# A three-layer cross network on one core: another order of GpSimd's additions, and other PSUM banks for ScalarE in layer 3

## The reference

```python
def cin_layer(xi, x0, W, b):            # xi (n, Fi, 32), x0 (n, 48, 32)
    Wr = W.reshape(Fi, 48, 128)
    out = einsum('nie,nje,ijo->noe', xi, x0, Wr) + b[None, :, None]
    return relu(out)
xs = [x0]
for W, b in ((W1, b1), (W2, b2), (W3, b3)):
    xs.append(cin_layer(xs[-1], x0, W, b))
z = concatenate(xs, axis=1).sum(axis=-1)
h = relu(concatenate([z, dense_ctx], 1) @ W_top1 + b_top1)
h = relu(h @ W_top2 + b_top2)
y = h @ W_top3
```

## Time and profile before

| | us |
|---|---|
| median of 3 runs (2476.27 to 2476.93) | 2476.67 |
| the profiled execution | 2476.69 |
| its span | 2474.9 |
| TensorE busy | 2330.4 (94%) |
| VectorE busy | 2277.5 (92%) |
| ScalarE busy | 2108.7 (85%) |
| GpSimd busy | 1904.7 (77%) |

### The profile page before, as it was taken

The page is one execution under the profiler, slowest core; times in us unless marked ns, Lnnn a source line. Parts: engine busy times, 40 slices in busy tenths (PEclk is TensorE's granted clock), DMA queues, the critical chain, the costliest instruction groups (busy, mean ns, idle before and its releaser), DMA issues.

```text
span 2474.9 us, 68697 instructions
## 1 busy us (share of the span) xinstructions
PE 2330.4 (94%) x14174; PEld 1177.3 (48%) x14174; DVE 2277.5 (92%) x9404; ACT 2108.7 (85%) x7910; POOL 1904.7 (77%) x1878
## 2 busy tenths in 40 slices
PE   1699999999999999999999999999999999999998
PEld 0355544454445544444454444444454555444443
DVE  6499999999999999999999999999999999999995
ACT  4589888898888988888988888888898898888884
POOL 7488888887778888888778888888777777777663
PEclk6799999999999999999999999999999999999999
DMA  5133333333333333333333333333333333333331
GB/s 168 28 69 71 70 70 62 70 71 68 60 70 70 71 61 70 71 65 66 69 68 71 66 66 70 67 64 70 67 66 64 69 69 68 68 61 68 68 60 37
DMA packets 150316, 168.61 MB, mean 68 GB/s; under 512 B 111956, under 2 KB 115671, under 8 KB 150264
## 3 DMA queue, kind: packets, MB, share of 16 engines
q0 software_dynamic: 43008, 137.39, 30.1%
q1 hardware_dynamic: 107256, 30.73, 5.6%
HBM read 12.82 MB, written 0.00 MB: 5 GB/s over the span
## 4 chain that ended last, share of the span: by engine, by line
DMA 23%; POOL 20%; PE 17%; ACT 16%; issue 13%; DVE 9%; DVEq 1%; ACTq 1%; POOLq 0%; SPq 0%
DMA work<-work 23%; PE y L469 13%; POOL part L346 12%; ACT work L567 11%; DVE acc L781 5%; POOL part L349 4%; PE m L459 3%; POOL psum L352 2%; ACT work L597 2%; POOL emb L294 2%; ACT zh L595 2%; DVEq L96 1%; ACT zst L592 1%; ACTq L96 1%; DVE mpw L822 0%
## 5 line engine op out<-in xcount | busy, mean ns | idle before, releaser
L469 PE MATMUL y<-whi,xT 128*128 128x512 f16 x6144 | 2009.5, 380 | 60.2 <-DVE acc L781 48.0
L567 ACT ACTIVATE work<-y,xc 128x128 f32<-128x128 f32 x5632 | 1600.6, 418 | 193.8 <-PE y L469 189.6
L781 DVE SCALAR_TENSOR_TENSOR acc<-y,xc,acc 128x128 f32<-128x128 f32 x5632 | 1650.6, 340 | 39.7 <-PE y L469 30.2
L469 PE MATMUL y<-wlo,xT 128*128 128x512 f16 x3072 | 1166.6, 380 | 0.0
L469 PEld LDWEIGHTS y<-whi,xT 128*128 128x128 f16 x6144 | 598.6, 97 | 721.5 <-issue 109.3
L346 POOL TENSOR_TENSOR part<-part,work 128x512 f32<-128x512 f32 x384 | 487.4, 1269 | 140.6 <-DMA work<-work 115.9
L469 PEld LDWEIGHTS y<-wlo,xT 128*128 128x128 f16 x3072 | 300.8, 98 | 223.1 <-issue 1.0
L357 POOL TENSOR_TENSOR zl<-work,zh 128x1152 f16<-128x1152 f32 x128 | 344.7, 2693 | 8.1 <-ACT work L597 8.1
L326 POOL DMA_DIRECT2D work<-work x256 | 229.0, 895 | 121.7 <-ACT work L567 120.8
L294 POOL DMA_INDIRECT emb<-tbl,ids_sb x192 | 202.3, 1054 | 45.1 <-issue 43.9
L346 POOL TENSOR_TENSOR part<-work 128x512 f32<-128x512 f32 x128 | 162.4, 1269 | 89.3 <-DMA work<-work 57.3
(11 more groups left out here) (102 smaller groups left out, 1877.7 us busy)
## 6 DMA issues: line engine op xcount, KB each, us to landing
work<-work POOLq DMA_DIRECT2D x256, 512.0 KB, 4.7
xT<-hi SPq DMA_TRANSPOSE x256, 3.2
xT<-lo SPq DMA_TRANSPOSE x256, 2.4
emb<-tbl,ids_sb POOLq DMA_INDIRECT x192, 2.6
xx<-w SPq DMA_DIRECT2D x4, 768.0 KB, 8.4
work<-w SPq DMA_DIRECT2D x4, 768.0 KB, 14.4
x0T<-x0hl SPq DMA_TRANSPOSE x128, 2.2
wt_sb<-W_top SPq DMA_DIRECT2D x1, 768.0 KB, 13.2
```

What stands on the lines that cost most here:

```text
L469: ins = nc.tensor.matmul(dst[:], xT[layer][:, parity, a, :], w[layer][:, cols], start=i == 0, stop=i == 2)
L567: nc.scalar.activation(prods[layer][:, a, k * P:(k + 1) * P], bank[:, k * P:(k + 1) * P], ACT.Copy, scale=xc[layer][:, parity, j:j + 1]).t ...
L781: ins = nc.vector.scalar_tensor_tensor(dst, y, col, mine, ALU.mult, ALU.add)
```

## The change

Two things change. First the order of GpSimd's additions. Before, the bank or banks that need no transfer are summed at 512 columns (`part`), and after the transfer's landing both landed banks are added to that at 512 columns, then folded to 256 and to 128. Now `sum_rest` also folds its sum to 256 columns, into a new tile `rest`, ahead of the landing; `sum_all` adds the two landed banks to each other (512), folds (256), adds `rest` (256), and folds to 128. For layer 3, `sum_rest` now waits for ScalarE's fifth bank, where it had nothing to do before. Second the table: in layer 3 ScalarE takes banks 0, 2, 4, 6, 8 (n = 12, 14, 16, 18, 20) in place of 1, 3, 5, 7, 9, and VectorE the other seven. `merge` of layer 2 moves with VectorE's banks from n = 20 to n = 21, and a reduction that is done in three of the last steps moves from n = 14 to n = 15.

```diff
--- before.py
+++ after.py
@@ -50,13 +50,13 @@
 HID1, HID2 = 512, 256
 
 
-TAKES = ("ADADADADADAD", "DADADADADADD")
+TAKES = ("ADADADADADAD", "ADADADADADDD")
 A_BANKS = [[n for n in range(BANKS) if t[n] == "A"] for t in TAKES]
 D_BANKS = [[n for n in range(BANKS) if t[n] == "D"] for t in TAKES]
 NA = [len(a) for a in A_BANKS]
 PRODS, FMAS = [Q * len(a) for a in A_BANKS], [Q * len(d) for d in D_BANKS]
 CHAINS = 2
-SUMS = [n - 1 for n in NA]
+SUMS = [n for n in NA]
 ADDED = 2
 CHUNKS = (1, 2, 0, 3)
 GATHERS, SPREAD, GROUP = 2, 8, 12
@@ -138,6 +138,7 @@
         xT = [sb(f"xT{l}", [P, 2, 2, P], f16) for l in (1, 2)]
         acc = [sb(f"acc{l}", [P, CHAINS * P]) for l in (2, 3)]
         part = [sb(f"part{l}", [P, Q * P]) for l in (2, 3)]
+        rest = [sb(f"rest{l}", [P, 2 * P]) for l in (2, 3)]
         psum = [sb(f"psum{l}", [P, P]) for l in (2, 3)]
         msum = [sb(f"msum{l}", [P, P]) for l in (2, 3)]
         tot = [sb(f"tot{l}", [P, 2]) for l in (1, 2)]
@@ -327,27 +328,31 @@
 
             def sum_rest(layer, tile):
 
-                wait(pool, s_sum[layer], tile * SUMS[layer])
+
+                s, n = s_sum[layer], tile * SUMS[layer]
+                a = prods[layer][:, 2 * ADDED, :]
+                wait(pool, s, n)
+                written(layer, tile, 2 * ADDED)
                 for m in range(2 * ADDED + 1, NA[layer]):
                     written(layer, tile, m)
-                    pool.tensor_tensor(part[layer][:], prods[layer][:, m - 1, :], prods[layer][:, m, :],
-                                       ALU.add).then_inc(s_sum[layer], 1)
+                    pool.tensor_tensor(part[layer][:], a, prods[layer][:, m, :], ALU.add).then_inc(s, 1)
+                    a = part[layer][:]
+                    n += 1
+                    wait(pool, s, n)
+                pool.tensor_tensor(rest[layer][:], a[:, 0:2 * P], a[:, 2 * P:4 * P], ALU.add).then_inc(s, 1)
 
             def sum_all(layer, tile):
 
-                s, n = s_sum[layer], tile * SUMS[layer] + NA[layer] - 2 * ADDED - 1
+                s, n = s_sum[layer], tile * SUMS[layer] + NA[layer] - 2 * ADDED
                 p, a = prods[layer], part[layer]
                 wait(pool, s_dma[layer], (tile + 1) * 16)
-                if NA[layer] == 2 * ADDED + 1:
-                    written(layer, tile, 2 * ADDED)
                 wait(pool, s, n)
-                for m in range(ADDED):
-                    rest = p[:, 2 * ADDED, :] if m == 0 and NA[layer] == 2 * ADDED + 1 else a[:]
-                    pool.tensor_tensor(a[:], rest, p[:, m, :], ALU.add).then_inc(s, 1)
-                    n += 1
-                    wait(pool, s, n)
+                pool.tensor_tensor(a[:], p[:, 0, :], p[:, 1, :], ALU.add).then_inc(s, 1)
+                wait(pool, s, n + 1)
                 pool.tensor_tensor(a[:, 0:2 * P], a[:, 0:2 * P], a[:, 2 * P:4 * P], ALU.add).then_inc(s, 1)
-                wait(pool, s, n + 1)
+                wait(pool, s, n + 2)
+                pool.tensor_tensor(a[:, 0:2 * P], a[:, 0:2 * P], rest[layer][:], ALU.add).then_inc(s, 1)
+                wait(pool, s, n + 3)
                 wait(pool, s_m[layer], tile)
                 pool.tensor_tensor(psum[layer][:], a[:, 0:P], a[:, P:2 * P], ALU.add).then_inc(s, 1)
 
@@ -868,13 +873,13 @@
                                 over_e(0, t1)
                         if n == 11 and k == 0 and active(t3 - 1):
                             over_e(2, t3 - 1)
-                        if n == 20 and k % 2 == 1 and active(t2):
+                        if n == 21 and k % 2 == 0 and active(t2):
                             merge(0, t2, k // 2)
                         if n == 22 and k == 0 and active(t1 + 1):
                             stacked_lo(t1 + 1)
                         if n == 23 and active(t2):
                             scale(1, t2, k)
-                    if n == 14 and isinstance(v, int) and TILES - NB <= v < TILES - 1:
+                    if n == 15 and isinstance(v, int) and TILES - NB <= v < TILES - 1:
                         x0_over_e(v - TILES + NB)
 
             steps(dve, step)
```

## The result

| | before | after |
|---|---|---|
| median of 4 runs | 2476.8 us (2476.27 to 2478.03) | 2512.41 us (2511.5 to 2513.13) |
| span of the profiled execution | 2474.9 | 2509.7 |
| ratio | | 1.0143 (95% interval 1.0125 to 1.016) |

What follows compares the result with a forecast made beforehand. It took a closed cycle of TensorE's n = 0 to n = 12 and ScalarE's packed 7.81 us as the bound. 123 steps by +0.03 = +3.7 us, all else 0, on 2476.69 gave 2480.4 us; range 2473 to 2506.

Steps and rivals of the forecast that it cites:

- The old chain: At a step's end: DMA landing, GpSimd's sum, VectorE's merge, TensorE's first bank; its 1.27 us wait all but goes.
- ScalarE's packed stretch: From n = 12 to its last product ScalarE never waits: five groups of products, three of squares, 7.81 us.
- TensorE's reaction: From the end of ScalarE's last product to TensorE's n = 0: 0.05 us in every step.
- the cycle: TensorE's n = 0 to bank n = 12, ScalarE's 7.81 us, next n = 0: mean step 18.34 us against 18.31.
- when ScalarE takes up n = 12: After n = 0: 10.38 to 10.50 us in odd steps, 10.51 in even ones, behind the x0 split.
- the lock: Beside n = 1 of even steps, VectorE's two-number L748 waits for GpSimd's whole instruction through a shared port pair; cost 0.
- rival B: The cycle is longer by little things, 0.1 us more a step: 2493 us; chance 0.18.
- L748 slips through just ahead: Even steps: L748 at 3.6 to 3.8 us after n = 0, new fold at 4.0, so L748 is not held.
- the case that I had drawn: In even steps with a gather, L748 comes just ahead of GpSimd's new fold, changing nothing in the cycle.
- A: The lock decides: fold or addition catches L748, even steps 19.0 us, +22 us (2502) to +37 (2517); chance 0.22.
- C: ScalarE's five groups close up, n = 20 is done in time, step 18.0 us, -38 us: 2439; chance 0.1.
- The pure forecast: 123 steps at +0.03 us, ends, GpSimd and VectorE 0: 2480.4 us, own range 2476 to 2485; chance 0.5.

Runs made afterwards that it cites:

- e2: The kernel before with the new table, merge and reduction moved to n = 21 and n = 15, GpSimd's additions as before: 2494.72 us, ratio 1.0062.
- e5: The changed kernel with VectorE's two operations on two numbers (L749, L753) each split into two on one number: 2497.62 us, ratio 1.0083.

## Why the prediction was wrong

**What held.** The old chain went, TensorE came to wait for ScalarE's n = 20 in nearly every step, and GpSimd's and VectorE's gains did not count. The loss per step, 0.44 us at n = 0 and 0.31 at n = 23, is near the 0.6 that was forecast for n = 0 alone. ScalarE's packed stretch was 7.81 in the prediction. An even step of the changed kernel, ScalarE's timeline (n = 10's scaling, n = 12's products, the last eight):

```profile
1565.17 0.37 ACT L616 ACTIVATE hi<-m,sc 128x128 f16<-128x128 f32 x1 [0.39 <-DVE mpw L827]
...
1566.84 1.16 ACT L572 ACTIVATE work<-y,xc 128x128 f32<-128x128 f32 x4
...
1572.39 2.25 ACT L572 ACTIVATE work<-y,xc 128x128 f32<-128x128 f32 x8
```

1572.39 + 2.25 - 1566.84 = 7.80 us. And TensorE, its n = 0 of this step and the next:

```profile
1556.04 0.39 PE L474 MATMUL y<-whi,xT 128*128 128x512 f16 x1 [0.28 <-ACT work L572]
...
1574.78 0.39 PE L474 MATMUL y<-whi,xT 128*128 128x512 f16 x1 [0.27 <-ACT work L572]
```

**First step that failed: TensorE's reaction.** ScalarE's last product ended at 1574.64, TensorE began at 1574.78: 0.14 us. I had taken 0.05, from one row near the start, another line, with a granted clock of 0.50 around it. So I gave the cycle 0.09 too little in every step: 123 x 0.09 = 11 us. In e2 it is 0.14 again (1652.45 + 2.24 to 1654.83):

```profile
1654.83 0.39 PE L469 MATMUL y<-whi,xT 128*128 128x512 f16 x1 [0.28 <-ACT work L567]
```

**Second: when ScalarE takes up n = 12.** The step from 1574.78 on, TensorE's n = 12 and next n = 0:

```profile
1584.78 0.59 PE L474 MATMUL y<-whi,xT 128*128 128x512 f16 x2
...
1593.22 0.39 PE L474 MATMUL y<-whi,xT 128*128 128x512 f16 x1 [0.27 <-ACT work L572]
```

and ScalarE's products of n = 12:

```profile
1585.28 1.14 ACT L572 ACTIVATE work<-y,xc 128x128 f32<-128x128 f32 x4
```

The bank was there at 1584.78 + 0.38 = 1585.16, 10.38 after n = 0, exactly as predicted. The products of n = 12 began 0.12 later. I had used 0.06, the middle of 0 and 0.12, although 0.12 was what the only row for it showed. Then 10.50 + 7.80 + 0.14 = 18.44, and the two n = 0 rows are 18.44 apart (ScalarE's marks 18.46). This adds 0.06 in odd steps, about 4 us. In even steps ScalarE began n = 12 a little later than my 10.51 even without the lock. In e5, with n = 0 at 1544.43:

```profile
1554.98 1.14 ACT L572 ACTIVATE work<-y,xc 128x128 f32<-128x128 f32 x4
```

That is 10.55, and makes some 2 us more. The late start at n = 12 in odd steps is rival B's mechanism; TensorE's reaction, the larger part, is not named in it, so that B's size of 0.1 a step was met is partly luck. e5, with the cycle and no lock, has a mean step of 18.474 for my 18.34, 16.5 us in all. In e2 only the first of the two is seen: 18.40 and 18.47 are my 18.30 and 18.37 with 0.10 more. Why ScalarE took up n = 12 sooner there stays open.

**Third: "L748 slips through just ahead".** It didn't. The same even step on VectorE:

```profile
1559.20 0.59 DVE L749 TENSOR_SCALAR mx<-mx 128x2 f32<-128x2 f32 x1
...
1559.96 0.58 DVE L753 TENSOR_SCALAR mp<-mx 128x2 uint32<-128x2 uint32 x1
```

and on GpSimd:

```profile
1558.69 1.07 POOL L295 DMA_INDIRECT emb<-tbl,ids_sb  x1 [0.17 <-issue]
1559.74 0.77 POOL L342 TENSOR_TENSOR rest<-work 128x256 f32<-128x256 f32 x1
```

L753 ended at 1560.54, just behind the fold's 1560.51. The gather's end came 4.58 after the transfer's issue at 1555.18, as worked out (4.57). But the issue was 0.86 ahead of n = 0 and not 0.7, and the fold followed the gather at once and not 0.1 later: 3.70 after n = 0 where I had 4.0. And L753 (before: L748) came at 3.92 where I had 3.6 to 3.8, since L749 ahead of it was held too, until 1559.79. The prediction has no term for L749 (before: L744), which ran free beside the gather in the step of the earlier trace rows (0.16 us at 1646.92). So it set a margin of 0.25 us between two estimates with errors as large, and called the slip likely. The delay reaches ScalarE's scaling (1565.17, after 0.39 of waiting): n = 12's products start at 10.80 after n = 0, not 10.51, and the even step is 18.74 where the cycle alone gives 18.49 (marks of e5).

Two of the 36 even steps with a gather show the case that I had drawn. In one of them n = 0 is at 400.13; VectorE and GpSimd:

```profile
403.29 0.16 DVE L749 TENSOR_SCALAR mx<-mx 128x2 f32<-128x2 f32 x1
...
403.62 0.47 DVE L753 TENSOR_SCALAR mp<-mx 128x2 uint32<-128x2 uint32 x1
...
402.98 1.07 POOL L295 DMA_INDIRECT emb<-tbl,ids_sb  x1 [0.17 <-issue]
404.03 0.77 POOL L342 TENSOR_TENSOR rest<-work 128x256 f32<-128x256 f32 x1
```

Here the fold comes 3.90 after n = 0 and L753 3.49. L753 is ahead of the fold, is held to the gather's end only (404.09 against 404.05), and the step takes 18.49: no loss.

**The long steps.** They are the even ones in which GpSimd moves gathered columns (L304). VectorE in one of them:

```profile
1184.94 2.09 DVE L749 TENSOR_SCALAR mx<-mx 128x2 f32<-128x2 f32 x1
...
1187.21 1.22 DVE L753 TENSOR_SCALAR mp<-mx 128x2 uint32<-128x2 uint32 x1
```

GpSimd:

```profile
1185.18 1.13 POOL L304 COPY xx<-emb 128x384 f32<-128x384 f32 x1
1186.00 1.00 POOL L342 TENSOR_TENSOR rest<-work 128x256 f32<-128x256 f32 x1
1187.14 1.26 POOL L350 TENSOR_TENSOR part<-work 128x512 f32<-128x512 f32 x1
```

and ScalarE:

```profile
1190.15 0.26 ACT L609 ACTIVATE m<-m 128x128 f32<-128x128 f32 x1 [2.40 <-DVE m L806]
```

L749 ended at 1187.03 with the fold (1187.00), L753 at 1188.43 with the addition (1188.40). GpSimd's instruction ahead of these (L362, the lower halves of the squares) ran from 1182.87 to 1185.54, so L749 waited out the rest of it, the copy and the fold, and L753 the addition: over 3 us for two numbers, and ScalarE stood idle 2.40. By the page "SBUF — State Buffer" of the Trainium skill, section "SBUF: two separate sides", whichever of GpSimd's operation and VectorE's operation in a two-port mode comes first has the shared port pair for its whole instruction, and the other blocks fully. The trace agrees to 0.03 us as to the end of the hold in these two places and at L753 above; the mode of an operation stands in no row. That L749 lost to three instructions in a row is read from this trace alone. Six such steps cost about 4 x 1.0 + 2 x 2.4 = 9 us, and 34 of the 36 steps with a gather 34 x 0.23 = 8: 17 us. Measured as a difference the lock is 14.8 us by e5 (16.6 by the mean steps of the two profiles, 18.609 and 18.474). e2 is 17.7 us below the changed kernel, but it lacks the fold too.

**The sum.** Predicted span 2474.9 + 3.7 = 2478.6; 11 us of TensorE's reaction, 6 of ScalarE's later n = 12, 17 of the lock give 2512.6; less the 1.2 and 0.6 by which the start and the end are shorter, 2510.8. Measured is 2509.7. (0.01 us in the reading of a step is 1.2 us here, so the sum can't be held to more than that.)

**The rivals.** A (22 to 37 us) and B (12) were each priced on their own, with 0.22 and 0.18. Neither excludes the forecast nor the other: the forecast's cycle, B's reactions and A's lock hold in the same step and add. Adding A's and B's prices gives 2480.4 + 22 + 12 = 2514 at the least, against 2512.4 measured; taking them as alternatives ended the range at 2506. A's own figure was high: the steps with a gather came to 18.7 and not 19.0, and only the six with moved columns went beyond. C is out: the stretch of 7.8 did not shorten. The pure forecast, 2480.4, was the cycle alone; e2 and e5 put that cycle at 2495 to 2498.

**What stays open.** Why L749 was held until the gather's end when the fold is the next instruction (1559.79 against 1559.76), and ran free beside a gather in the kernel before, in e2 (1658.04 for 0.15 us, gather from 1657.48 to 1658.55) and at 403.29 of the changed kernel, where the fold follows the gather at once too. It began 0.31 us after the gather's start at 403.29 (free), 0.51 at 1559.20 (held) and 0.56 in e2 (free), so neither the place within the gather nor the instruction behind it tells by itself. The halves of the split were not tried apart either. And no run says why the RECIPROCAL on the same two numbers is never held.

## What to carry to other kernels

When a chain is removed, price the cycle that takes its place with reactions read in the steady part, between the same two engines and on the same line; 0.1 us in every step is as much as a whole stall in some. Rivals that can hold at once must be added before the range is set. An operation of VectorE on a few numbers that lasts much longer in the median than at its best is worth a look for its own sake: here splitting two of them in the kernel before gave 29 us, and with the merge moved two banks later 66. A line of waits that is added up over the run need not be the wait that one looks for: it has to be laid over the program's own count first.

## What the runs showed of the hardware

- A VectorE TENSOR_SCALAR on 128 x 2 numbers in SBUF took 151 to 158 ns when free and up to 2.1 us beside GpSimd; on 128 x 1 it took 142 ns on the mean and was not held (e5).
- The width is not all: the RECIPROCAL behind it, on 128 x 2 numbers too, was never held, though it ran beside GpSimd's additions (1560.72, addition from 1560.65 to 1561.92). All of its executions (ns min/median/max, first and last start):

```profile
L758 DVE RECIPROCAL sc<-mp x64: 145/150/166, 68.3 to 2377.4; 128x2 f32<-128x2 f32 x64
```

- ScalarE to TensorE took 0.14 us in the steady steps, against 0.05 in the earlier trace rows; TensorE to ScalarE 0.12 at 1585.28, as in the earlier trace rows.
- A held operation ended 0.03 us behind GpSimd's instruction, and one waited out parts of three of them (2.09 us).
